# ScalarE loads the exponential's table in front of the copy of attention's transpose

## The reference, cut to what matters

```
x = x + layernorm(attention(layernorm(x)))     # 16 heads of 8
    q, k = exp(xn@Wq.T + bq), exp(xn@Wk.T + bk);  v = xn@Wv.T + bv
    out  = (q . cumsum(k v)) / (q . cumsum(k));   out @ Wo.T + bo
x = x + layernorm(slot_mixture(layernorm(x)))  # 8 experts of 64 slots = 512 slots
    logits = rms(x) . rms(slot_embeds)
    dispatch = softmax over experts; slots = dispatch^T x
    h = gelu(slots @ w1);  processed = h @ w2
    combine = softmax over all slots;  out = combine processed
```

## Time and profile before

| | |
|---|---|
| median of 3 runs | 649.88 us (646.66 to 650.04) |
| the profiled execution's own time | 648.46 us |
| its span, first to last instruction | 646.7 us |
| PE, PEld busy | 92%, 80% of the span |
| DVE, ACT, POOL busy | 74%, 69%, 76% |
| table loads: line 504, line 455, line 469 | 38, 32 and 3, each 1283 ns |
| mean granted clock of TensorE | 0.994 |

### The profile page before, as it was taken

How to read it: one execution, slowest core, us unless ns; L and a number is a source line. 1 busy time by engine, 2 the same in 40 slices (tenths; PEclk the granted TensorE clock), 3 DMA queues, 4 the chain that set the end, 5 groups by cost and what they waited for, 6 DMA issues and landing times.

```text
span 646.7 us, 12987 instructions
## 1 busy us (share of the span) xinstructions
PE 591.8 (92%) x4136; PEld 520.5 (80%) x4136; DVE 480.2 (74%) x929; ACT 444.8 (69%) x1065; POOL 488.9 (76%) x501
## 2 busy tenths in 40 slices
PE   2446899999999999999999999999999999999886
PEld 1235788889888888889888888889888888888875
DVE  6877778777778778777778778777778778767521
ACT  3224777777777777777777777777777777777755
POOL 4998788888888888888888888888888888873100
PEclk9998999999999999999999999999999999999989
DMA  3000000000000000000000000000000000000000
GB/s 105 9 13 12 17 10 17 26 26 26 26 26 17 26 10 26 26 26 25 26 26 18 26 10 24 27 26 26 26 26 16 26 10 26 17 26 9 9 10 17
DMA packets 16838, 14.44 MB, mean 22 GB/s; under 512 B 2850, under 2 KB 16644, under 8 KB 16772
## 3 DMA queue, kind: packets, MB, share of 16 engines
q1 hardware_dynamic: 14708, 12.76, 6.6%
q10 hardware_dynamic: 2064, 0.86, 0.5%
HBM read 5.25 MB, written 4.19 MB: 15 GB/s over the span
## 4 chain that ended last, share of the span: by engine, by line
PE 81%; DVE 6%; POOL 5%; issue 4%; ACT 2%; DMA 0%; SPq 0%; DVEq 0%; POOLq 0%; ACTq 0%
PE HB L710 16%; PE LA L692 9%; PE LA L721 9%; PE HB L562 6%; PE LA L672 5%; PE HB L564 4%; PE HB L563 4%; PE WB L642 3%; DVE WB L926 3%; PE HB L700 3%; PE WB L643 3%; PE WB L562 3%; PE LB L681 2%; PE WB L625 2%; PE WB L591 2%
## 5 line engine op out<-in xcount | busy, mean ns | idle before, releaser
L710 PE MATMUL HB<-w_c,hid 128*128 128x128 f32 x1024 | 125.5, 277 | 0.8 <-ACT hid L411 0.8
L710 PEld LDWEIGHTS HB<-w_c,hid 128*128 128x128 f32 x1024 | 122.0, 193 | 1.2 <-issue 1.2
L411 ACT ACTIVATE hid<-HB 128x512 f32<-128x512 f32 x128 | 76.5, 598 | 31.8 <-PE HB L564 28.4
L906 DVE TENSOR_TENSOR prod<-WB,E 128x1024 f32<-128x1024 f32 (+1 forms) x96 | 90.7, 944 | 6.4 <-PE WB L643 5.8
L310 POOL TENSOR_TENSOR kv<-E 128x1024 f32<-128x1024 f32 x32 | 68.5, 2141 | 31.4 <-ACT E L404 31.2
L926 DVE TENSOR_REDUCE WB<-prod 128x288 f32<-128x2304 f32 x32 | 81.9, 2561 | 7.6 <-DVE xnT_lo L892 7.2
L318 POOL TENSOR_TENSOR kv_lo<-kv,kv_hi 128x1152 fp32r<-128x1152 f32 x32 | 85.2, 2662 | 0.0
L371 POOL TENSOR_TENSOR kv<-kv,kv_prev 128x1024 f32<-128x1024 f32 x32 | 76.5, 2390 | 0.0
L310 POOL TENSOR_TENSOR kv_prev<-prev 128x1024 f32<-128x1024 f32 x32 | 68.3, 2133 | 0.1
L692 PE MATMUL LA<-xn,disp 128*128 128x129 f32 x512 | 62.5, 275 | 0.9 <-ACT disp L404 0.9
L721 PE MATMUL LA<-proc,comb 128*128 128x129 f32 x512 | 62.5, 275 | 0.7 <-ACT proc L404 0.7
(11 more groups left out here) (134 smaller groups left out, 1506.3 us busy)
## 6 DMA issues: line engine op xcount, KB each, us to landing
X<-in_L_attn_x_dram SPq DMA_DIRECT2D x32, 128.0 KB, 2.1
out_dram<-res SPq DMA_DIRECT2D x32, 128.0 KB, 1.9
prev<-E SPq DMA_DIRECT2D x32, 112.0 KB, 2.1
w_in<-in_L_ffn_w_dram ACTq DMA_DIRECT2D x2, 256.0 KB, 4.5
prev<-E SPq DMA_DIRECT2D x32, 15.0 KB, 2.0
se_in<-n_L_ffn_slot_embeds_dram ACTq DMA_DIRECT2D x1, 256.0 KB, 3.9
w_in<-in_L_attn_Wq_dram SPq DMA_DIRECT2D x1, 64.0 KB, 2.4
w_in<-in_L_attn_Wk_dram SPq DMA_DIRECT2D x1, 64.0 KB, 2.2
```

Of the source, the lines that this page charges most:

```text
L411: act.activation(hid[:, f, :], HB[:, f % 2, :], ACT.Gelu).then_inc(gelu_ready[f], 1)
L710: last = pe.matmul(PR[:, j, :], hid[:, f, j * P:(j + 1) * P], w2_c[:, f, :], start=(f == 0), stop=(f == FJ - 1))
L906: dve.tensor_tensor(prod[u][:, :, d0 * DIM:d1 * DIM].rearrange("p c (d f) -> p c d f", d=g), WB[:, k % 2, 0:g * DIM].rearrange("p (o d f) ...
```

## The change

One line is added to ScalarE's step, between the output's squares and the copy of attention's transpose. It writes out a load of the exponential's table there.

More of the change, by code:

```diff
@@ L516, in step @@
                     o_squares(a)
+                act.preload_act_table(ACT.Exp)
                 if r is not None:
```

## The result

| | before | after |
|---|---|---|
| median of 4 runs | 648.95 us (646.66 to 650.04) | 672.05 us (671.29 to 672.88) |
| profiled execution: own time, span | 648.46, 646.7 | 672.88, 671.1 |
| copy to copy, full steps | 18.19 us | 18.99 us |
| mean granted clock of TensorE | 0.994 | 0.972 |

The change makes the kernel slower: ratio 1.0361, 95% interval 1.0325 to 1.0396. It was forecast as 671.5 us.

The account below looks back on a forecast made before the run. TensorE's queue was taken as the bound, with 81% of the chain that ended last. Terms 20.8 + 0.3 + 1.95 - 0.4 - 0.5 + 0.3 = 22.45 us gave 670.9 to 672.3, forecast 671.5 us, range 659 to 679.

Parts of the forecast that it names:

- The full steps: Steps 1 to 27: the load makes attention's copy 0.80 us late, TensorE loses 0.77 us a step, 20.8 us in all.
- weights hidden in a shorter matmul: Project's second half: part of 0.11 us for exposed weights may hide in a 384-column matmul, so 0.77 and not 0.79.
- a gap of 0.15 us: TensorE's wait ahead of the next cumulated sums might take some delay back; lower bound 0.62 us a step.
- The start: Five loads and not one ahead of the first xT_hi make the whole start slip; 1.95 us, bounds 0 to 3.5.
- Steps -1 and 0: Step 0 loses some 0.3 us at the copy; step -1 hides the load and gains 0.4 us by an earlier Exp.
- The last steps: Dispatch exponentials no longer wait for the load but for neg_max; 0.17 us each, 0.5 us back in three steps.
- The end: Three loads and not one follow the last squares on ScalarE; 0.3 us more.
- A: A load ahead of a copy of PSUM costs one more load's length, 35 us on top, 706 us; 1 in 100.
- B: TensorE loses its clock at the new stall; at least 22 us more, 693 us or higher; 4 in 100.
- C: TensorE does not feel the late copy or makes it up within the step; 650 us; 7 in 100.
- E: The wait is partly felt, 0.3 to 0.6 us a step; 657 to 666 us; 10 in 100.
- D: The chain from the Exp sets the step, so 0.44 us a step would go; 636 us; 3 in 100.

Follow-up runs that it names:

- the start alone: Changed kernel, with the load of the exponential's table written out only in the first two steps; 651.16 us, ratio 1.0048.
- the split kernel with the early load: Changed kernel, with one tile of process moved between project's two halves on TensorE; 659.65 us, ratio 1.0168.
- short dose: Kernel before, with one 200-column copy into a spare buffer ahead of attention's copy in steps 0 to 27, no load moved; 649.31 us, ratio 1.0014.
- split with the load behind: Kernel before, load still behind the copy, with one tile of process between project's two halves; 656.52 us, ratio 1.0134.
- last-steps kernel: Kernel before, with the load written out only in steps 28 to 30; 647.82 us, ratio 0.9997.
- three loads: Kernel before, with three table loads (exponential, gelu, exponential) ahead of the copy in steps 0 to 27; 802.76 us in one run.
- squares behind: Changed kernel, with the load only in steps 0 to 27 and the output's squares moved behind the copy; 656.52 us, ratio 1.0138.

## Why the prediction was right

- **Bound and mechanism.** TensorE waits for the copy in 28 steps, and nothing in the loop gives it back. The full steps were reckoned at 0.77 us and took 0.80; 27 of them 21.5 us and not 20.8. The copy's delay was right; what I took off for weights hidden in a shorter matmul was wrong, and so was the idea that a gap of 0.15 us might take some back: the same gap is there ahead of the cumulated sums after.
- **The start.** 1.95 reckoned. The copy of step -2 starts at 41.19 and not at 39.23: 1.96. The mechanism is as said, but that the number fits so well is luck. It was reckoned from, and is compared with, the one execution in which before itself was late; against the seven others, in which this copy starts at 38.46 to 38.60, it is 2.6 to 2.7.
- **Steps -1 and 0.** Reckoned 0.3 for step 0 less 0.4 for step -1; in the profiled executions they lost 2.6 us, so this term of the sum was wrong. The copy of step 1 starts at 98.77 and not at 93.37, 5.40 late, of which 0.80 are its own step's and 1.96 the start's. Two more executions, both at a granted clock of 1.00 over 57 to 77 us, take this apart. From the copy of step -2 to that of step 1 the kernel before takes 54.14 us, the start alone 54.83, the split kernel with the early load 55.88 and the changed kernel 57.58.
  - 1.7 us are the clock: the changed kernel's was 0.68 over 57 to 77 us, and the split kernel with the same loads had 1.00. It is not the change's doing. Without an early load in these steps the same stretch has 0.74 (short dose) and 0.66 (split with the load behind), with it in full steps only, 1.00.
  - 0.7 us lie between before and the start alone, whose work in these steps is the same, and although before's clock was 0.91 there. TensorE's transposes of attention in step -1 took 0.44 us in before and 0.69 in the other, both at a granted clock of 1.00. Why stays open.
  - 0.3 us are step 0's, as reckoned: 19.00 us from the copy of step -1 to that of step 0 in the split kernel, 18.72 in the start alone. This leaves nothing of the gain of 0.4 us in step -1. It rested on before's execution: in both of these the Exp of that step starts at 61.13 and waits for project, with the load ahead or behind.
- **The last steps.** Reckoned 0.5 us back, and 0.6 came: the dispatch exponentials of steps 28 to 30 are 25.94, 25.72 and 25.52 us late (612.35, 629.40 and 646.24), the copy of step 27 was 26.13. They wait for neg_max as said:

```profile
646.24 1.57 ACT L469 ACTIVATE disp_t<-LB,neg_max 128x256 f32<-128x256 f32 x4 [1.40 <-DVE neg_max L971]
```

- After them 1.64 us more came back, by the last squares (666.38 against 642.50, 23.88 late). Before, the clock fell there; after, it is 1.00 over 645 to 650 us. I had not put that in the sum. The last-steps kernel shows that an early load does not prevent it.
- **The end.** 0.3 reckoned, 0.5 found: the last load ends at 669.60 + 1.28 = 670.88, and the span is 671.1.

The sum after the fact is 1.96 + 2.64 + 21.53 - 0.61 - 1.64 + 0.52 = 24.40, against 24.42 between the two profiled executions. Medians differ by 23.1. The prediction's sum was 22.45 us, and it came so near by luck in part: it put nearly nothing at the 2.64 of steps -1 and 0 and nothing at the 1.64 that came back behind the last exponentials, and the second cancels the greater part of the first. What it forecast with its reasons, the 27 full steps, is 21.53 of the 24.40.

- **Rivals.** A, a hidden price of a load: the rows around each load of the full steps have 0.01 to 0.02 us on either side, and at the start one load follows the other after 1.29 us; out. B, the clock: out at this length, real at 3.1 us. C and E, not or only partly felt: out by the table above. D, the Exp leads the loop: out, but its margin is smaller than I wrote. "No TensorE instruction of a full step waits for what follows from the Exp" holds only while v's copy is less than 0.3 us later, as the split showed.

## What to carry to other kernels

Ask of a table load not how long it is but who waits for what stands behind it: it belongs ahead of the instruction whose reader has the most time, which here was the Exp. An engine's idle time ahead of an instruction covers only its own length (0.50 of 1.30 us here), and beyond it an instruction that is just in time for the bounding engine passes its delay on in full, in every step. A load written out in a pipeline's step also runs in the steps that have no use for it: here four more ahead of the first work, 2.0 to 2.8 us.

## What was not expected of the hardware

The mean granted clock differs between executions of one kernel. The changed kernel took 671.3 us in the two executions with a mean of 1.0 and 672.8 in the two with 0.97. In the profiles the difference lies in the start, 0.66 to 1.00 over 57 to 77 us, and in three of them (after, short dose, three loads) 0.50 over 39 to 57 us. The length of one wait does not tell whether the clock falls. In step -1 TensorE waited 1.44 us ahead of the part's transposes in before and with the squares behind; the granted clock fell to 0.50 in the first and stayed at 1.00 in the second. Near the end it fell behind waits of 2.24 us (before) and 2.05 us (last steps alone), but not behind one of 2.04 us (after). With one of 3.1 us in every full step it fell in all but one: 21.57 us there, 23.9 in most others.
